# Output projection of the global attention moved to the end of the kernel, weight splits moved into the global stage, local and gated orders changed

## The reference

```python
xn = layernorm(x)
s = global_attention(xn)          # 16 heads of 16, causal, rotary; ends in out @ Wo.T + bo
g = silu(local_ffn(xn))           # 2 layers of the following
x = x + s * g

# one local layer
h = shift_token(x)                # second half of the channels comes from the token before
q, k, v = split(h @ wqkv)         # 8 heads of 64, l2norm, scales, rotary with xpos
x = x + window_attention(q, k, v) @ wo      # blocks of 128, the own block and the one before
h = layernorm(shift_token(x)) * lg + lb
a, g = split(h @ w1 + b1)         # 682 hidden
x = x + (a * gelu(g)) @ w2 + b2
```

## Time and profile before

| what | us |
|---|---|
| median of 3 runs (lowest, highest) | 3438.68 (3431.89, 3445.53) |
| the profiled execution, its own time | 3436.42 |
| its span, first to last instruction | 3434.6 |
| PE busy | 3019.9 (88%) |
| DVE busy | 2397.2 (70%) |
| ACT busy | 1715.1 (50%) |
| POOL busy | 977.9 (28%) |

### The profile page before, as it was taken

How to read it: one execution, slowest core, us unless ns; L and a number is a source line. 1 busy time by engine, 2 the same in 40 slices (tenths; PEclk the granted TensorE clock), 3 DMA queues, 4 the chain that set the end, 5 groups by cost and what they waited for, 6 DMA issues and landing times. The chain is left out here.

```text
span 3434.6 us, 75969 instructions
## 1 busy us (share of the span) xinstructions
PE 3019.9 (88%) x31408; PEld 1860.6 (54%) x31408; DVE 2397.2 (70%) x4022; ACT 1715.1 (50%) x3173; POOL 977.9 (28%) x1011
## 2 busy tenths in 40 slices
PE   7799999999999999999868999957987899985796
PEld 6443333334433333344457777746776777764675
DVE  7699999986879997875246666645655666663555
ACT  4277777887768888888223333312223333321222
POOL 7410000000110000001135555522435555542333
PEclk9799999999999999999989999988998999997898
DMA  7520001000020000000220000001000000003001
GB/s 241 141 63 17 9 9 46 9 9 17 25 69 17 9 9 10 5 8 8 92 72 20 20 18 17 33 7 48 18 23 26 14 21 20 15 27 115 22 19 51
DMA packets 76866, 121.77 MB, mean 35 GB/s; under 512 B 9478, under 2 KB 41220, under 8 KB 75908
## 3 DMA queue, kind: packets, MB, share of 16 engines
q1 hardware_dynamic: 72452, 110.94, 10.6%
q10 hardware_dynamic: 4096, 6.30, 0.7%
HBM read 74.47 MB, written 33.55 MB: 31 GB/s over the span
## 5 line engine op out<-in xcount | busy, mean ns | idle before, releaser
L652 DVE TENSOR_REDUCE mp<-ps_m 128x2 f32<-128x1024 f32 (+3 forms) x1152 | 1275.0, 1134 | 188.3 <-PE ps_m L703 131.2
L630 ACT ACTIVATE probs<-ps_s 128x512 f32<-128x512 f32 (+3 forms) x2304 | 1162.3, 561 | 368.1 <-PE ps_s L727 335.0
L743 PE MATMUL ps_o<-probs,vall 128*32 128x256 f32 (+3 forms) x9216 | 703.5, 377 | 15.9 <-POOL probs L607 9.6
L727 PE MATMUL ps_s<-qst,kst 64*128 64x512 f32 (+3 forms) x2304 | 590.6, 481 | 5.4 <-ACT probs L630 4.1
L703 PE MATMUL ps_m<-kst,qst 64*128 64x512 f32 (+3 forms) x2304 | 478.8, 399 | 33.9 <-DVE mp L652 16.4
L727 PEld LDWEIGHTS ps_s<-qst,kst 64*128 64x128 f32 x2304 | 239.5, 185 | 454.8 <-ACT probs L630 398.2
L743 PEld LDWEIGHTS ps_o<-probs,vall 128*32 128x32 f32 x9216 | 184.4, 108 | 337.6 <-issue 174.3
L703 PEld LDWEIGHTS ps_m<-kst,qst 64*128 64x128 f32 x2304 | 231.9, 191 | 78.6 <-DVE mp L652 59.3
L596 POOL TENSOR_TENSOR msplit<-negm,mzero 128x16 fp32r<-128x16 f32 x32 | 7.2, 225 | 902.6 <-DVE negm L658 902.6
L1022 POOL TENSOR_TENSOR a_rot<-a_scr 128x512 f32<-128x512 f32 x128 | 163.7, 1279 | 322.4 <-DVE a_scr L1378 322.4
L607 POOL TENSOR_SCALAR_AFFINE_SELECT probs<-probs 128x256 f32<-128x256 f32 x256 | 103.5, 409 | 504.6 <-ACT probs L630 504.5
(11 more groups left out here) (187 smaller groups left out, 5263.3 us busy)
## 6 DMA issues: line engine op xcount, KB each, us to landing
a_tab<-in_rope SPq DMA_DIRECT2D x32, 512.0 KB
q_parts<-pparts SPq DMA_DIRECT2D x32, 256.0 KB, 4.2
k_parts<-pparts SPq DMA_DIRECT2D x32, 256.0 KB, 3.9
qst<-q_parts SPq DMA_DIRECT2D x64, 128.0 KB, 2.7
o_raw<-o_sb SPq DMA_DIRECT2D x32, 256.0 KB, 2.1
X<-in_x SPq DMA_DIRECT2D x8, 512.0 KB, 6.2
kst<-k_parts SPq DMA_DIRECT2D x32, 128.0 KB, 4.0
qst<-q_parts SPq DMA_DIRECT2D x64, 64.0 KB, 2.6
```

What stands on the lines that cost most here:

```text
L630: act.activation(probs[:, s % PR, h, off:C], sslots[n % SR][:, off:C], ACT.Exp, scale=float(D) ** -0.5).then_inc(exp_done, 1)
L652: dve.tensor_reduce(mp[b % 2][:, h:h + 2, cc:cc + 1], slot[:, :, 0:width], AX.X, ALU.max).then_inc(max_read, 1)
L727: pe.matmul(sslots[n % SR][:, off:C], kst[g % 2][rows, hp, i * P:(i + 1) * P], qst[q_slot(b)][rows, hp, off:C], start=True, stop=True).the ...
L743: last = pe.matmul(ps_o[32 * h:32 * h + VW, lo:hi], vall[:, i, (g * GH + h) * DV:(g * GH + h) * DV + VW], probs[:, s % PR, h, lo:hi], star ...
```

## The change

- `project_out` is gone. Its spreading, weighing and projecting now stand in `gate`, chunk by chunk, together with the product with SiLU(X) and the sum with x. What it loads (`w_o`, `b_o`, `o_raw`, x: 34 DMAs, kept in `ahead`) is loaded during the second `mlp_layer`, five DMAs after each `shifted(sp, k)`. The reciprocal and its split, and the selector, are made in that layer's last slot. The spreading uses fp32r products with high and low parts where it used one fp32 product. `gate` takes SiLU into X in place.
- The first local layer's qkv and output weights are loaded and split in the last quarter of `global_attention`: eight pieces of 512 columns, one per block, with a load from SP, a copy on ACT and a subtraction on POOL each. They lie in `keep`, the memory of the keys of the groups 0 and 2. The first local layer no longer loads and splits its output weights.
- `local_attention_layer`: on PE, the output projection of pair k-4 stands between the q/k projections 0 and 1 (at the slot's end for k of 16 and up), `turn_max(2k-3)` ahead of the norms' transposes, `turn_max(2k-2)` ahead of `score_turned(2k-4)`, and `weigh(k-3, 0)` ahead of the transposes of the sums of squares. ACT's copy for `turn_max(2k-2)` moves ahead of the exponentials of window 2k-4.
- `mlp_layer`: the 127-partition DMA becomes one of 112 and one of 15. A chunk is measured at the end of the slot before and normalized within the first two gated blocks. The low part of the last hidden block (42 rows) goes from POOL to DVE. Loads for later stages are issued after `shifted(sp, 1)` and the following ones.

```diff
-def project_out(nc, y_rows, o_raw, w_o, b_o, ident, w_next, W):
...
# global_attention
+        split_at = {first_step[3 * NC + p] + 3: p for p in range(NC)}
+        pool_order = sorted(pool_order + [(2 * s + 3, 2, p) for s, p in split_at.items()])
...
+                if s in split_at:
+                    p = split_at[s]
+                    (hi, _), at = w_pieces[p]
+                    act.wait_ge(w_in, 16 * (p + 1))
+                    act.activation(hi[:, at:at + C], w_f[:, :], ACT.Copy).then_inc(w_high, 1)
# local_attention_layer, PE
+                if win(2 * k - 3):
+                    turn_max(2 * k - 3)
                 if live(k - 1):
...
                 if live(k):
                     project(k, 0)
+                    project_out(k - 4)
                     project(k, 1)
...
+                if win(2 * k - 2):
+                    turn_max(2 * k - 2)
                 if win(2 * k - 4):
                     score_turned(2 * k - 4)
...
-                if win(2 * k - 2):
-                    turn_max(2 * k - 2)
+                if live(k - 3):
+                    weigh(k - 3, 0)
                 if live(k):
                     pe.wait_ge(sse_done, k + 1)
                     for a in range(2):
                         last = pe.transpose(B6[:, a * P:(a + 1) * P], sse[:, a * P:(a + 1) * P], id_sb[:, :])
                     last.then_inc(sst_done, 1)
-                if live(k - 3):
-                    weigh(k - 3, 0)
+                else:
+                    project_out(k - 4)
# mlp_layer
-            sp.dma_start(xs[1:P, :, P:E], X[0:P - 1, t:t + TPC, P:E]).then_inc(xs_in, 16)
+            sp.dma_start(xs[1:Q + 1, :, P:E], X[0:Q, t:t + TPC, P:E]).then_inc(xs_in, 16)
+            sp.dma_start(xs[Q + 1:P, :, P:E], X[Q:P - 1, t:t + TPC, P:E]).then_inc(xs_in, 16)
...
-            if ahead:
-                sp.wait_ge(ahead_in, 16 * len(ahead))
-
+            share = -(-len(ahead) // (NC - 1))
             for k in range(1, NC):
                 sp.wait_ge(hn_done, TPC * k)
                 shifted(sp, k)
+                if k == 1 and w_next is not None:
+                    sp.dma_start(w_f[:, :], w_next).then_inc(next_in, 16)
+                for dst, src in ahead[(k - 1) * share:k * share]:
+                    sp.dma_start(dst, src).then_inc(ahead_in, 16)
+            if ahead:
+                sp.wait_ge(ahead_in, 16 * len(ahead))
...
+                if live(c):
+                    for m in range(HC):
                         gated(c, m)
+                        if live(k) and m < 2:
+                            normalize(k, 2 * m)
+                            normalize(k, 2 * m + 1)
...
+                if live(k + 1):
+                    measure(k + 1)
+                    aggregate(k + 1)
# gate, PE
+                    pe.matmul(ps_d[n % 4][:, :], rows, rec_hi[:, :], start=True, stop=False)
+                    pe.matmul(ps_d[n % 4][:, :], rows, rec_lo[:, :], start=False, stop=True).then_inc(spread_done, 1)
```

More of the change, by code:

```diff
@@ L45 @@
 WCOLS = EC * 2 * HP
+WOCOLS = INNER // P * E
 def repeat(eng, n, body):
@@ L975, in _ @@
                 sp.dma_start(tab[:, :, :], rope[:, k, :, :]).then_inc(tab_in, 16)
-                if k == 0:
+                if k == 0 and w_o is not None:
                     sp.dma_start(stage[:, :], w_o).then_inc(wo_in, 16)
@@ L1250, in weigh, with project_out @@
                 last.then_inc(av_done, 1)
+            def project_out(p):
+                if live(p):
+                    if p == 0 and w_o is not None:
+                        pe.wait_ge(wl_done, 1)
+                    pe.wait_ge(olo_done, 2 * p + 2)
+                    pe.wait_ge(rec_done, 2 * p + 2)
+                    if live(p + 4):
+                        pe.wait_ge(vc_done, 2 * (p + 4) + 1)
+                    for a in range(2):
+                        tok = slice(a * P, (a + 1) * P)
+                        for j in range(OC):
+                            last = product3(pe, B6[:, a * E:(a + 1) * E], oT_hi[:, j, tok], oT_lo[:, j, tok], wo_hi[:, j, :],
+                                            wo_lo[:, j, :], j == 0, j == OC - 1)
+                    last.then_inc(wo_done, 1)
             for k in range(NI + 4):
@@ L1444, in _, with mlp_layer @@
                 divide(k - 3, 0)
-def mlp_layer(nc, layer, X, W, w_next, ahead, w_2, b_1, ln_cols, ident):
+                if not live(k):
+                    add_out(k - 4)
+def mlp_layer(nc, layer, X, W, w_next, ahead, sums, w_2, b_1, ln_cols, ident):
     with ExitStack() as ctx:
@@ L1709, in slot @@
                     dve.tensor_tensor(W[1][:, :], w_f[:, :], W[0][:, :].bitcast(F32), ALU.subtract).then_inc(next_low, 1)
+                if isinstance(k, int) and k == NC and sums is not None:
+                    den, rec_hi, rec_lo, sel = sums
+                    dve.wait_ge(ahead_in, 16 * len(ahead))
+                    dve.reciprocal(den[:, :], den[:, :]).then_inc(rec_done, 1)
+                    dve.wait_ge(rec_done, 1)
+                    dve.wait_ge(rec_high, 1)
+                    dve.tensor_tensor(rec_lo[:, :], den[:, :], rec_hi[:, :].bitcast(F32), ALU.subtract).then_inc(rec_low, 1)
                 if live(c):
@@ new lines, in _, with spread @@
+        @block.tensor
+        def _(pe):
+            def spread(c):
+                for e in range(2):
+                    n = 2 * c + e
+                    if n >= 4:
+                        pe.wait_ge(on_done, n - 3)
+                    rows = sel[:, H * c + HH * e:H * c + HH * e + HH, :].rearrange("p m o -> p (m o)")
+                    pe.matmul(ps_d[n % 4][:, :], rows, rec_hi[:, :], start=True, stop=False)
+                    pe.matmul(ps_d[n % 4][:, :], rows, rec_lo[:, :], start=False, stop=True).then_inc(spread_done, 1)
+            spread(0)
+            for c in range(NC):
+                if c + 1 < NC:
+                    spread(c + 1)
+                pe.wait_ge(on_done, 2 * c + 2)
+                for b in range(2):
+                    n = 2 * c + b
+                    if n >= 4:
+                        pe.wait_ge(y_out, n - 3)
+                    for a in range(2):
+                        tok = slice((2 * b + a) * P, (2 * b + a + 1) * P)
+                        for e in range(2):
+                            last = pe.matmul(ps_y[n % 4][:, a, :], on[:, c % 2, e, tok], wo_sb[:, e, :], start=(e == 0), stop=(e == 1))
+                    last.then_inc(y_done, 1)
```

321 lines of the change are left out of this document (126 added, 195 removed).

## The result

The changed kernel takes 3252.66 us (median of four runs, 3251.14 to 3260.36), the kernel before beside it 3441.3 us (four runs as well, 3431.89 to 3445.53). The ratio is 0.946, with a 95% interval of 0.9434 to 0.9486. The profiled execution took 3260.36 us with a span of 3258.6 us and is the slowest of the four; it is 176.0 us of span shorter than the profiled execution of before.

The account below looks back on a forecast made before the run. PE and its gaps bound most stages; `project_out` and `gate` cost time without PE as limit. From 3436.4 us, -68.1 + 15.3 - 27.6 - 27.7 - 27.6 - 18 - 24 + 2.4 = -175.3 gives 3261, median 3262; range 3228 to 3300.

Parts of the forecast that it names:

- likeliest case: Full local slots: DVE gets between POOL's instructions, 0.5 to 1.5 us a slot won, 3250 to 3274 us; chance 0.40.
- rival A: Full local slots: POOL's trims do not shut DVE out, 2.1 us a slot won, 3236 us; chance 0.22.
- rival B: Full local slots: DVE is shut out until L994 ends, +0.2 us a slot, 3291 us; chance 0.29.
- part 6: Local pipeline's drain and fill: 8 of PE's 14.0 us waits won, 1 us in the fill, twice; -18 us.
- part 7: Full local slots, 24 in all: moves cover PE's waits, 1.0 us a slot; -24 us, bounds -50 and +5.
- Part 1: `project_out` removed: its whole stretch falls away, its loads hide in the second `mlp_layer`; -68.1 us.
- Part 2: `gate` grows from 27.7 to 43.0 us, with PE setting the pace at 4.4 us a chunk; +15.3 us.
- rival C: `gate`: PE runs the stage at the lower clock, +35 us, 3297 us; chance 0.05.
- Part 3: Start of each `mlp_layer`: the trickling 127-partition transfer and stuck SP issue go, 13.8 us a layer; -27.6 us.
- Part 4: Second slot of each `mlp_layer`: PE's waits of 3.6 and 22.9 us for hidden values go; -27.7 us.
- Part 5: Full `mlp_layer` slots: early normalizing and the last low part leaving POOL end PE's waits; -27.6 us, bounds 20 to 28.
- Part 8: Global stage: eight ACT copies for the weight splits cost 0.3 us each; +2.4 us, bounds 0 and 5.

Follow-up runs that it names:

- e3_pool_order: Changed kernel, in full local slots POOL's first trim moved ahead of `rn` and its low part held until DVE split both maxima; 3227.8 us, ratio 0.939.
- e0_after: The changed kernel timed again with no edit; 3258.65 us, 0.9485 of the kernel before.
- e11_spread_f32: Changed kernel with the spreading products of `gate` in fp32 instead of fp32r; 3273.26 us, ratio 0.9546.
- e8_before_split: Kernel before, with only the shifted rows' 127-partition transfer split into 112 and 15 partitions; 3364.61 us, ratio 0.9777.
- e9_last_pool: Changed kernel with the low part of the last hidden block computed by POOL again; 3265.77 us, ratio 0.9495.
- e4_drain: Changed kernel, in the local drain ACT's last weights moved ahead of the high part and POOL's trims ahead of the low part; 3244.72 us, ratio 0.9444.

## Why the prediction was right, and where its terms were wrong

The total was forecast at 3262 us and is 3252.66, inside the likeliest case's 3250 to 3274 us. The case was also right in its mechanism: DVE is shut out by POOL's trims and gets in between POOL's instructions. It was not right in its size: the slot of 30.9 us is the one that the forecast gave for rival A (30.8), and only L1267's 0.64 us, and not 0.17, tells the two apart. Rival A (no lockout) and rival B (lockout until L994's successor ends) are both refuted by the slot's timeline and by e3_pool_order; C by a granted clock of 0.93 in `gate`; D by the 0.76 us of the one-row DMA; E by a kernel that got faster and slots that got shorter. But the sum came out well partly by luck, because terms of opposite error met in the local attention: part 6 was 24 us too good and part 7 21 us too small.

The forecast named two signs of being wrong. The first, waits that the old order did not have, does not show in the full slots, though it does in the drain (part 6). The second, a global stage longer by more than 5 us, did show in the profiled execution (7.4 us), but it was a poor sign: one kernel's global stage differs by 9 us from one execution to another (e0_after).

**Part 1** was right: the stage is gone, and the work behind the shifted transfers costs no wait of PE in the second `mlp_layer`, whose 215.15 us are the first one's 215.91.

**Part 2** was +15.3 and is +17.0. The 4.4 us a chunk are 4.38. The missing 1.7 us are about what the start costs: PE fell to the lower clock just behind the barrier, so that the first eight spreads take 3.14 us (3217.82 - 3214.68) where eight at 0.23 take 1.84, and the first projection 0.4 us more than the others. The forecast knew the case only as rival C, for all of the stage. One aside of it was wrong: "four fp32 spreading instructions" in the earlier trace rows were two, each in two records (and the sixteen projecting ones eight), so a spreading instruction took 0.86 us, and fp32 spreads for high and low parts would have cost 20 us more, not 6 (e11_spread_f32).

**Part 3** was right: -13.8 a layer, measured -14.2 (18.55 to 4.36 us). Of these the two narrow transfers make 12.4 (to 6.14 us in e8_before_split), and 1.8 come from VectorE's wait for the constants, which is gone too; the forecast had put all of it on the transfer.

**Part 4** was right in its 26.5 us of waits: both are gone. Its reading of the second layer is half right: SP's wait for `y_rows` and x makes 10.9 us, the transfer the other 12.0 (e8_before_split). The 1.2 us for the lower clock fit the trace: behind the 22.9 us the products stand 0.43 us apart for some 3 us.

**Part 5** had the right size and a wrong cause. "The chunk is normalized early, so the transposes should not wait" and "the last low part leaves POOL": the 15.1 and 12.5 us do go, but in the old order two narrow transfers take them away without either move. In the new order the low part had to leave POOL: put back there, it is late again, held up by VectorE (e9_last_pool). The forecast took the trickle for a cost at the starts and in the second slots, and did not ask what a transfer of 13.7 us with SP stuck behind it does in each slot of 27. The parts 3 to 5 together were 82.9 us and measured 92.6. The waits removed are 14.2 x 2 + 26.5 + 27.6 = 82.5 us; nearly all of the other 10 is PE's own work, 4.1 and 5.3 us shorter in busy time (205.87 to 201.75 and 207.20 to 201.86) at a granted clock of 0.96 for 0.94 and 0.90. The forecast had put 1.2 us on this.

**Part 6** failed: -18 forecast, +5.5 in the profiled executions, and no gain in any run. In the first layer the distance from the last `rn` to the stage's end went from 80.9 to 85.4 us, and the way from the stage's start to the fourth `rn` from 99.1 to 99.4. In the second layer the same two went from 85.3 to 85.5 and from 99.4 to 99.7. So the new order lengthened them by 4.9 us in one layer and by 0.6 in the other, and most of that is the clock of one drain. The first layer's two drains, before and after:

```profile
2224.90:2305.80 80.90, 57.81 (x1074) 48.11 (x1062) 38.08 (x80) 17.98 (x23) 31.00 (x31) 0.92 0.05 21
```

```profile
2141.87:2227.27 85.40, 60.95 (x1006) 49.86 (x998) 38.72 (x80) 18.17 (x23) 31.60 (x31) 0.84 0.04 15
```

PE's waits in them are 21.4 and 22.8 us; the other 3.1 us are busy time at the lower granted clock. In the six traced drains of the old order these waits are 20.8 to 21.4 us, and 22.8 in all ten of the new one: what the order itself does is 1.4 to 2 us more of waiting, whatever the clock. The step that failed is "I take 8 of the 14 us". PE's wait for the low parts did fall by 9.4 us, since other products stand before them. But "some waits come back" was larger than the gain. POOL's low part of k-4 stands ahead of the trims, and ACT's high part ahead of the last weights, as they did before; PE stood in its wait for the low part meanwhile. Now it comes to `weigh` first and waits 6.1 us for a trimmed tile, with more behind it. e4_drain changes nothing but these queues and wins 6.8 us a layer.

**Part 7** was -24 and is -45: 1.9 us a slot instead of 1.0. The mechanism was as forecast, the size was not: it lies outside the 0.5 to 1.5 us of the likeliest case. PE's waits fell from 2.9 to 1.45 us, and 0.4 us lie in PE's own products and small gaps (297.78 us busy in 327 before, 294.44 in 309 after). The step is "Between these ends I take 1.0 us a slot": with the mechanism that I called likeliest, 1.5 remain by my own working, and this is what the waits show (2.9 - 1.45); I had mixed rival B's loss into the likeliest case's number.
The Trainium skill ("SBUF — State Buffer", Who interferes with whom) says that, where a VectorE instruction in a two-port mode meets GpSimd, whoever issues first gets the shared ports for the whole instruction and the other waits. The trace agrees for the trims: 0.64 and 0.55 us beside trims of 0.63, 0.18 without them. It does not agree for POOL's power instruction `rn` of 5.44 us: the same two DVE instructions ran within it in 0.173 to 0.177 us, four of each in the changed kernel, and 17 and 4 of them in e3_pool_order.

**Part 8** was +2.4 and cannot be told from nothing: PE's wait for ACT's copies is 1.7 us in seven times, as in the earlier trace rows, the nine executions with the copies end the stage at 1665.5 us in the mean and the two without at 1664.7 and 1668.3. The +7.4 are the profiled execution's own, with PE's busy time and clock as the difference found (e0_after).

What stays open: what of the 18 us of waits that e4_drain leaves in the drain is a chain of dependences that no order can shorten, and what decides the clock there: drains with nearly the same waits (20.8 to 22.8 us) were granted 0.82 to 0.92, two of one execution 0.92 and 0.84. That part of up to 5 us a layer was seen and not explained.

## What to carry to other kernels

A transfer that trickles (here 19 GB/s, at a DMA share of 0.09) holds up every transfer issued behind it in each repetition: look for its tail in the steady slots' waits, not only where it is the last releaser by name. When instructions are moved on one engine, follow the queues of the engines that serve it through the fill and the drain as well as through the full slot, since a low part that is hidden there can stand ahead of what PE needs next. Where a stage comes twice in the kernel, read both before a difference of a few us is put down to an order: here the first layer's drain alone was 4 us shorter than the second's, in the same program. And if the likeliest mechanism has a price by its own working, sum with that price and keep the rivals' prices for the range.

## What the runs showed of the hardware

- Trims on POOL (128x512, one input, in place, 0.63 us) shut out DVE instructions on 128x8 elements until the trim ends, 0.64 and 0.55 us for 0.18 (26 of 64 pairs in the changed kernel, none in e3_pool_order).
- The other direction: a subtraction on POOL (42x512) beside two copies and two subtractions of 128x512 on DVE took 2.93 us where these took their usual time (the kernel before, e9_last_pool), and 1.40 where the second copy took 1.5 us instead of 0.41 (e8_before_split).
- POOL's power instruction of 5.44 us (128x32) did not shut out the same DVE instructions: those within it took 0.173 to 0.177 us (eight in the changed kernel, 21 in e3_pool_order).
- A product of 512 columns took 0.86 us in fp32, recorded twice, and 0.23 in fp32r, at the full clock in both; the fp32 projections of 256 columns beside them, eight a chunk, stand as sixteen records 0.22 us apart in both kernels.
- After a pause of 2.26 us at `gate`'s barrier PE was at the lower clock from about 3215.2 to 3218.6 (spreads 0.43 us apart), though it had come from a stretch granted 0.96.
- The global stage of one kernel took 1661.0 to 1672.1 us in nine profiled executions, with PE's busy time and clock as the only difference found. Where the code is the same, the first `mlp_layer` repeats within 0.6 us (215.4 to 215.9), the new order's local attention takes 553.6 to 556.0 us, and the old order's 573.0 to 577.8.
